# Three blocks of a two-layer kernel joined into one, with row products moved into the value products

## The chip, the cores and the metric

The kernel runs on one core of a Trainium2 chip. The metric is the device time of one execution in microseconds (us). Five engines run programs of their own and meet at semaphores: PE (TensorE, matrix products), DVE (VectorE), ACT (ScalarE), POOL (GpSimd) and SP (SyncE, which here only issues DMA transfers). PE's weight loads are shown apart as PEld.

## What is computed

Two layers act on 1024 tokens (2 sequences of 512) of width 512. The first adds attention and a gated feed-forward network to its input, the second a state-space mixer and a linear map with LoRA. Both normalise first.

```python
x = L0_attn_x                                   # (2, 512, 512), float32
xn = _layernorm(x)
q, k, v = proj(w_q), proj(w_k), proj(w_v)       # 32 heads of 16
attn = softmax(q @ k.T / 4)
inter = silu(xn @ gate_w.T * gate_scale) * (xn @ up_w.T * up_scale)      # width 1376
x = x + (attn @ v) @ w_o.T + inter @ down_w.T * down_scale
xn = _layernorm(x)
proj = xn @ in_proj_w.T                         # gate, x, B, C, dt
xBC = silu(conv1d(xBC, 4 taps) + conv_b)
y = ssd(xBC, dt, A, D)                          # 128 heads of 64, state 128, 8 groups, chunked scan
g = y * silu(gate)
g = g * rsqrt(mean(g * g over each group) + 1e-5) * norm_w
x = x + g @ out_w.T + (xn @ W.T + bias + lora(xn))
```

## The kernel before

**Products.** Each float32 product of weights and activations is made as three passes at reduced width: both operands are split into a high part (ACT copies, `hi`) and a rest (DVE or POOL subtracts, `lo`), and `product` issues hi times lo, lo times hi and hi times hi on PE (L156, L157, L158). Weights come by DMA into `raw` slots of a `Feed` and are split there (high L137 on ACT, rest L148 on DVE or POOL).

**Stages.** Three blocks follow one another, each with a program for each engine, and each ends with all five engines together. `emit_qkv` normalises the input and projects q, k and v. `emit_attention` runs the attention in a loop of 2 iterations of 4 quads (a quad is 4 heads in both sequences), with the gate and up products between its steps. `emit_ssm` first runs the program of `Down` (feed-forward down projection, attention output, second normalisation) and then 8 groups of the state-space part in 16 steps each; the last group differs a little, and behind it comes the output stage (`Output`, and the last products with `out_w`). On each engine the order of work is the order in which the code issues it; no scheduler moves it.

**The first normalisation** (`FirstNorm`) goes over 8 blocks of 128 tokens (`NTOK`). For block t DVE takes the moments (L242, L244), ACT a square root, DVE inverts it and forms a shift, ACT normalises in place, PE turns the block with four transposes (L210) into PSUM, ACT copies the high part (`xhi`, L227) and DVE the rest (`xlo`, L255). In an iteration t, ACT does the root of t, the normalisation of t-1 and the high part of t-2; DVE the moments of t, the scalars of t-1 and the rest of t-2.

**The projections.** A q or k tile is a weight block by both halves of the tokens (`half(n, b)`, 12 matmuls each). The first half of tile 0 begins once four blocks are split; the last three turns stand around it and the first half of tile 1 on PE. A finished q or k tile is copied to DRAM (`parts`, SP L427) and read back re-arranged as `stk_qs` and `stk_ks`, 12 transfers for each of four quads (`stack`, SP L329). SP issues these between the loads of the v weights (L129).

**The value products.** v takes 8 steps t of 12 matmuls each (`qkv_pv`). After each step PE does two row products of the first quads (`row_step`, L341, four matmuls in all), whose maxima DVE takes (L351). Row products have two buffers.

**The state-space part.** SP fetches running sums (`cumb`, 1 MB, `sums`) for each step; POOL splits weight rests (L148), decays the state (L1863), gates the output (L1875), adds up squares (L1881, L1885) and weighs inputs for the state (`ssm_xw`, L1852), which PE then needs (L1437). The sum of squares of a group goes over PE (L1421) to DRAM and back as a reciprocal root (`rstd`), by which the output stage scales the gated rows (DVE L2099), splits them (ACT L2066, DVE L2103) and multiplies them with `out_w`.

## Time and profile before

| | us |
|---|---|
| median of 3 runs | 2115.75 (2115.68 to 2117.44) |
| profiled execution, own time | 2119.49 |
| its span | 2117.8 |
| PE busy in it | 2077.2 (98%) |
| DVE, ACT, POOL busy | 1464.2, 1336.9, 868.3 |

The profile page tells one execution. It gives the busy time of each engine, then what each engine waited for, then single instructions in time. PE is the engine to follow here, and what matters is where it does not work or works at a lower clock.

### The profile page before, as it was taken

What the parts mean: (1) busy time and instruction counts of PE and PEld (TensorE: products, weight loads), DVE (VectorE), ACT (ScalarE), POOL (GpSimd) and SP (SyncE); (2) the same over time, 40 slices, a digit from 0 to 9 for tenths busy, and PEclk for the clock granted to TensorE, in tenths of its full rate; (3) what the DMA queues carried; (4) which work ended last, traced back from release to release, by engine and by line L of the source; (5) the groups of instructions that cost most, each with busy time, mean ns of one, the idle gap of its engine ahead of it and who ended that gap; (6) DMA issues with size and microseconds to landing.
All of it is one profiled execution on the core that took longest, in us unless ns stands there. A gap on an engine that the chain in (4) does not pass through costs nothing.

```text
span 2117.8 us, 33682 instructions
## 1 busy us (share of the span) xinstructions
PE 2077.2 (98%) x12040; PEld 1547.6 (73%) x12040; DVE 1464.2 (69%) x1811; ACT 1336.9 (63%) x2376; POOL 868.3 (41%) x762
## 2 busy tenths in 40 slices
PE   7899999999999999999999999999999999999999
PEld 5644444488877777777877777777777767888887
DVE  4466666286578778878778687787787775555555
ACT  4255555544678888878787887888778783233322
POOL 1001110131266666757667566676667681000000
PEclk9999999999999999999999999999999999999999
DMA  4422222142455545545455455455555457544552
GB/s 156 163 80 73 76 80 60 46 153 88 135 159 168 164 142 172 157 154 173 154 158 162 147 166 168 151 167 159 153 168 159 155 174 267 151 145 147 147 182 89
DMA packets 182781, 305.34 MB, mean 144 GB/s; under 512 B 20416, under 2 KB 96704, under 8 KB 182496
## 3 DMA queue, kind: packets, MB, share of 16 engines
q1 hardware_dynamic: 182624, 303.29, 46.3%
q8 instruction: 94, 1.54, 0.3%
q14 instruction: 63, 0.52, 0.1%
HBM read 249.90 MB, written 53.06 MB: 143 GB/s over the span
## 4 chain that ended last, share of the span: by engine, by line
PE 76%; ACT 1%; DVE 1%; POOL 1%; issue 1%; DMA 1%; DVEq 0%; SPq 0%; POOLq 0%; ACTq 0%
PE ssm_pp L156 16%; PE ssm_pp L158 15%; PE ssm_pp L157 15%; PE ssm_py L1458 5%; PE ssm_py L1453 4%; PE ssm_pstate L1437 4%; PE ssm_turn L1414 2%; PE ssm_py L158 1%; PE ssm_py L157 1%; PE ssm_py L156 1%; PE down_ps L156 1%; PE down_ps L158 1%; PE down_ps L157 1%; PE ssm_pp L1397 1%; PE ssm_pstate L158 1%; PE ssm_pstate L157 1%
## 5 line engine op out<-in xcount | busy, mean ns | idle before, releaser
L156 PE MATMUL ssm_pp<-xhi,ssm_lo 128*128 128x512 f32 x1192 | 478.8, 402 | 0.9 <-DVE ssm_bc L1697 0.4
L158 PE MATMUL ssm_pp<-xhi,ssm_hi 128*128 128x512 f32 x1192 | 465.5, 391 | 0.0
L157 PE MATMUL ssm_pp<-xlo,ssm_hi 128*128 128x512 f32 x1192 | 464.9, 390 | 0.0
L1583 ACT ACTIVATE ssm_sct<-ssm_cumb,ssm_gpar 128x128 f32<-128x128 f32 x1024 | 313.1, 390 | 71.5 <-DMA ssm_cumb<-dt_sums 50.3
L148 POOL TENSOR_TENSOR ssm_lo<-ssm_raw,ssm_hi 128x512 fp32r<-128x512 f32 x150 | 244.0, 1631 | 79.1 <-ACT ssm_hi L137 79.1
L156 PEld LDWEIGHTS ssm_pp<-xhi,ssm_lo 128*128 128x128 f32 x1192 | 223.6, 188 | 63.7 <-issue 18.8
L1697 DVE SCALAR_TENSOR_TENSOR ssm_xc<-ssm_pp,vectors,ssm_xc 128x1022 f32<-128x1022 f32 (+2 forms) x192 | 245.3, 1278 | 28.0 <-ACT ssm_xc L1537 23.4
L158 PEld LDWEIGHTS ssm_pp<-xhi,ssm_hi 128*128 128x128 f32 x1192 | 223.7, 188 | 48.1
L157 PEld LDWEIGHTS ssm_pp<-xlo,ssm_hi 128*128 128x128 f32 x1192 | 224.0, 188 | 42.6
L1732 DVE TENSOR_TENSOR ssm_sct<-ssm_sct,ssm_cbm 128x1024 f32<-128x1024 f32 x128 | 228.5, 1785 | 27.7 <-ACT ssm_sct L1590 27.7
L1875 POOL TENSOR_TENSOR ssm_go<-ssm_t,ssm_gt 128x512 f32<-128x512 f32 x128 | 165.0, 1289 | 171.8 <-DVE ssm_t L1768 171.8
L767 ACT ACTIVATE att_pt<-att_keys 128x512 f32<-128x512 f32 x256 | 143.8, 594 | 137.3 <-PE att_keys L657 137.1
L2066 ACT ACTIVATE xlo<-ssm_gt 128x1024 fp32r<-128x1024 f32 x64 | 67.8, 1060 | 239.4 <-PE ssm_turn L158 228.1
L351 DVE TENSOR_REDUCE stk_mx<-att_rows 128x2 f32<-128x1024 f32 x112 | 137.3, 1226 | 90.2 <-PE att_rows L341 90.2
L148 POOL TENSOR_TENSOR ffn_lo<-ffn_raw,ffn_hi 128x512 fp32r<-128x512 f32 x33 | 42.9, 1301 | 377.1 <-ACT ffn_hi L137 377.1
L1744 DVE TENSOR_TENSOR ssm_xp<-ssm_turn,ssm_gpar 128x512 f32<-128x512 f32 x128 | 87.9, 687 | 151.9 <-PE ssm_turn L1414 151.9
L1458 PE MATMUL ssm_py<-ssm_sct,ssm_xp 128*64 128x128 f32 x2048 | 184.3, 274 | 0.0
L2103 DVE TENSOR_TENSOR xlo<-ssm_gt,xlo 128x1024 fp32r<-128x1024 f32 x64 | 78.4, 1225 | 149.1 <-ACT xlo L2066 149.1
L1852 POOL TENSOR_TENSOR ssm_xw<-ssm_xp,ssm_gpar 128x512 f32<-128x512 f32 x96 | 127.1, 1324 | 107.7 <-DVE ssm_xp L1744 107.6
L1453 PE MATMUL ssm_py<-ssm_cecl,ssm_state 128*64 128x128 f32 x1536 | 154.1, 279 | 0.1
L1768 DVE SCALAR_TENSOR_TENSOR ssm_t<-ssm_xc,vectors,ssm_py 128x128 f32<-128x128 f32 x512 | 142.5, 338 | 5.3 <-PE ssm_py L1458 5.3
L1458 PEld LDWEIGHTS ssm_py<-ssm_sct,ssm_xp 128*64 128x64 f32 x2048 | 124.5, 137 | 24.3 <-DVE ssm_xp L1744 18.2
(287 smaller groups left out, 4148.3 us busy)
## 6 DMA issues: line engine op xcount, KB each, us to landing
ssm_cumb<-dt_sums SPq DMA_DIRECT2D x96, 1024.0 KB, 5.9
ssm_raw<-w SPq DMA_DIRECT2D x150, 256.0 KB, 5.4
gated<-ssm_go SPq DMA_DIRECT2D x128, 256.0 KB, 4.3
ssm_cumb<-dt_sums SPq DMA_DIRECT2D x32, 512.0 KB, 3.9
ssm_gt<-w SPq DMA_DIRECT2D x64, 256.0 KB, 2.7
ssm_xc<-gated SPq DMA_DIRECT2D x32, 512.0 KB, 4.1
ssm_sct<-gated SPq DMA_DIRECT2D x32, 512.0 KB, 4.2
ffn_raw<-w SPq DMA_DIRECT2D x37, 256.0 KB, 2.8
```

Source lines behind the costliest of these rows:

```text
L148: i = dve.tensor_tensor(lo, src, hi, ALU.subtract)
L156: pe.matmul(out, wlo, xhi, start=start, stop=False)
L157: pe.matmul(out, whi, xlo, start=False, stop=False)
L158: return pe.matmul(out, whi, xhi, start=False, stop=stop)
L767: act.activation(pt[:, kt % 2, PAIRED[u % HQ], :], keys[:, u % 2, :], ACT.Exp).then_inc(exp_done, 1)
L1453: pe.matmul(p_y[r * HP:(r + 1) * HP, s % 2, ct, :], state[:, ch % 2, h * HP:(h + 1) * HP], cecl[:, s % 2, h, :], start=True, stop=False)
L1458: mm = pe.matmul(p_y[r * HP:(r + 1) * HP, s % 2, ct, :], xp[:, s % 2, h * HP:(h + 1) * HP], sct[:, s % 2, h, :], start=(ch == 0), stop=True)
L1583: i = act.activation(sct[:, s % 2, h, :], cumb[:, s % 2, 0, h, :], ACT.Relu, scale=-1.0, bias=gpar[:, unit, 0, s % NTOK, h:h + 1])
L1697: i = dve.scalar_tensor_tensor(dst[:, :, sh:L], pp[:, e % 2, :, 0:L - sh], col(conv_col(g, e) + tap), dst[:, :, sh:L], ALU.mult, ALU.add)
L1732: dve.tensor_tensor(sct[:, s % 2, :, :], sct[:, s % 2, :, :], cbm[:, s % NTOK, :].unsqueeze(1).broadcast_to([P, HU, CS]), ALU.mult).then_i ...
L1768: i = dve.scalar_tensor_tensor(t2[:, s % 2, ct, :], xc[:, s // NTOK, ct, t * CS:(t + 1) * CS], col(g * (2 * CU) + (V_D + s // NTOK * CU + ...
L1875: pool.tensor_tensor(go[:, s % 2, :, :], t2[:, s % 2, :, :], gt[:, s // NTOK, :, t * CS:(t + 1) * CS], ALU.mult).then_inc(g_done, 1)
```

## The change

**One block.** `emit_qkv` becomes a class `Projections`, `emit_attention` a class `Attention`; their engine programs are called at the head of each engine's program in `emit_ssm`'s block, ahead of `Down`. In place of the two joint ends stand waits on semaphores: for all value copies on PE and POOL, for the last value sums and the last transfers of q and k parts on DVE, for these transfers on ACT; and in `Down` for the last copied attention sums on SP and, within its first tile, for that and the last gate and up tile on PE. Semaphores of the projections are given back (`retired`) before those of the state-space part are taken.

**First normalisation.** In an iteration ACT now does the high part of t-3, the normalisation of t-1 and the root of t; DVE the scalars of t-1, the moments of t and the rest of t-3. On PE six turns come first, the seventh stands within the first half of tile 0 and the eighth behind it.

**Order on SP.** The stacks move behind all loads of the v weights:

Here is SP in the projections; `qkv_raw` is a v weight, L427 a copy to DRAM, L329 the stacks. Before:

```order
L427 DMA qk_parts<-qk_lo 128x1024
L329 DMA stk_qs<-qk_parts 16x2x512 x6
L329 DMA stk_ks<-qk_parts 16x2x512 x6
L129 DMA qkv_raw<-w 128x512
L427 DMA qk_parts<-qk_hi 128x1024
L427 DMA qk_parts<-qk_lo 128x1024
L329 DMA stk_qs<-qk_parts 16x2x512 x6
L329 DMA stk_ks<-qk_parts 16x2x512 x6
L129 DMA qkv_raw<-w 128x512
```

And after, where the copy to DRAM has L423:

```order
L129 DMA qkv_raw<-w 128x512
L423 DMA qk_parts<-qk_hi 128x1024
L423 DMA qk_parts<-qk_lo 128x1024
L329 DMA stk_qs<-qk_parts 16x2x512 x6
L329 DMA stk_ks<-qk_parts 16x2x512 x6
L423 DMA qk_parts<-qk_hi 128x1024
L423 DMA qk_parts<-qk_lo 128x1024
L329 DMA stk_qs<-qk_parts 16x2x512 x6
L329 DMA stk_ks<-qk_parts 16x2x512 x6
```

Each stack (12 transfers) has moved from between two v weights to behind the last of them; the third now also stands behind two loads for the attention's gate and up weights.

**Row products.** The two row products of step t are done inside its value product, after the first 3 of 12 matmuls; only those of t = 0 still stand behind it. Here is PE at the end of the value products and the start of the attention. Before:

```order
L156 MATMUL qkv_pv<-qkv_hi,xlo 128x512
L157 MATMUL qkv_pv<-qkv_lo,xhi 128x512
L158 MATMUL qkv_pv<-qkv_hi,xhi 128x512
L341 MATMUL qkv_ps<-stk_ks,stk_qs 128x512 x4
L398 UNCONDITIONAL_BRANCH
L647 UNCONDITIONAL_BRANCH
L341 MATMUL att_rows<-stk_ks,stk_qs 128x512 x2
L657 MATMUL att_keys<-stk_qs,stk_ks 128x512 x2
```

After:

```order
L158 MATMUL qkv_pv<-qkv_hi,xhi 128x512
L341 MATMUL qkv_ps<-stk_ks,stk_qs 128x512 x4
L156 MATMUL qkv_pv<-qkv_hi,xlo 128x512
L157 MATMUL qkv_pv<-qkv_lo,xhi 128x512
L158 MATMUL qkv_pv<-qkv_hi,xhi 128x512
...
L156 MATMUL qkv_pv<-qkv_hi,xlo 128x512
L157 MATMUL qkv_pv<-qkv_lo,xhi 128x512
L158 MATMUL qkv_pv<-qkv_hi,xhi 128x512
L341 MATMUL att_rows<-stk_ks,stk_qs 128x512 x2
```

The last row products have moved ahead of nine matmuls of the last value step, and the attention's first row products follow the value product with no change of block between them.

**Running sums.** The transfer of `cumb` for a step waits for two ACT marks (`seg_done`, `cecl_done`) that show its buffer read, and no longer for the state of the step before (`st_done`).

**Last group and output.** SP loads the first inputs of the output stage at step 11 (before at 14) and asks for the first reciprocal roots at step 14 (before 15). Four weight rests go from POOL to DVE (`low_beside`). From step 6 on POOL weighs before it adds squares. ACT's last square and PE's last sums of squares move a few instructions into the output stage. Here is POOL near the end of the last group, before:

```order
L1852 TENSOR_TENSOR ssm_xw<-ssm_xp,ssm_gpar 128x512
L148 TENSOR_TENSOR ssm_lo<-ssm_raw,ssm_hi 128x512
L1863 TENSOR_TENSOR ssm_state<-ssm_state,ssm_cdec 128x512
L1875 TENSOR_TENSOR ssm_go<-ssm_t,ssm_gt 128x512
L1881 TENSOR_TENSOR ssm_sq<-ssm_sq 128x256
L1885 TENSOR_TENSOR ssm_sqs<-ssm_sq 128x128
L1852 TENSOR_TENSOR ssm_xw<-ssm_xp,ssm_gpar 128x512
```

And after:

```order
L1894 TENSOR_TENSOR ssm_state<-ssm_state,ssm_cdec 128x512
L1906 TENSOR_TENSOR ssm_go<-ssm_t,ssm_gt 128x512
L1883 TENSOR_TENSOR ssm_xw<-ssm_xp,ssm_gpar 128x512
L1912 TENSOR_TENSOR ssm_sq<-ssm_sq 128x256
L1916 TENSOR_TENSOR ssm_sqs<-ssm_sq 128x128
```

The weighing (L1852, now L1883) has moved ahead of the two additions of squares, and the weight rest (L148) is gone from the row.

The core of the diff:

```diff
 class FirstNorm: def scalar(self, act, feed):
-        for t in range(NTOK + 2):
+        for t in range(NTOK + 3):
+            if t >= 3:
+                self.high(act, t - 3)
+            if 1 <= t <= NTOK:
+                self.normalise(act, t - 1)
             if t < NTOK:
                 self.root(act, t)
-            if 1 <= t <= NTOK:
-                self.normalise(act, t - 1)
-            if t >= 2:
-                self.high(act, t - 2)
-            if 4 <= t < 4 + feed.begun:
-                feed.split_hi(act, 0, t - 4, 0)
+            if 3 <= t < 3 + feed.begun:
+                feed.split_hi(act, 0, t - 3, 0)
 ...
 SP of the projections
-                if n == 1:
-                    for s in parts_out[0:2]:
-                        sp.wait_ge(s, 32)
-                    sp.wait_ge(st.cleared, 2)
-                if 1 <= n < NB:
-                    st.stack(sp, c, 0, n - 1)
 ...
+            for s in parts_out[0:2]:
+                sp.wait_ge(s, 32)
+            sp.wait_ge(st.cleared, 2)
+            for i, n in enumerate(range(3 * KT - S - 2, nqk)):
+                st.stack(sp, c, 0, i)
                 parts(n)
             next_feed.begin_load(sp)
+            st.stack(sp, c, 0, NB - 2)
             st.neg_max(sp, 0, 0)
 ...
 PE of the projections
-            for t in range(NC + 1):
+            for t in range(NTOK - 2):
                 norm.turn(pe, t)
             pe.wait_ge(norm.lo_done, NC)
-            half(0, 0)
-            norm.turn(pe, NC + 1)
-            norm.turn(pe, NC + 2)
+            half(0, 0, range(KT // 2))
+            norm.turn(pe, NTOK - 2)
+            half(0, 0, range(KT // 2, KT))
+            norm.turn(pe, NTOK - 1)
             half(1, 0)
-            norm.turn(pe, NC + 3)
             pe.wait_ge(norm.lo_done, NTOK)
 ...
                     if t == 0:
                         pe.wait_ge(feed.lo_done, nqk + k + 1)
+                    if t > 0 and k == 1:
+                        maxima(t)
 ...
 heads of the engine programs of the attention
+            projections.values_out(pool)
             sweep(pool, body)
+            projections.values_out(pe)
             sweep(pe, body)
+            projections.vectors_in(dve)
+            projections.values_summed(dve)
+            projections.parts_written(dve)
+            projections.parts_written(act)
             act.wait_ge(scale_set, 3)
 ...
 Down
+            attention.last_sums_copied(sp)
             move_sums(sp, c, oe, att_moved, NIT - 1, NB - 1)
 ...
+                    if k == 0 and t == 4:
+                        attention.last_sums_copied(pe)
+                    if k == 0 and t == 6:
+                        attention.last_tile_read(pe)
 ...
 emit_ssm
             def sums(g, s):
-                after(sp, st_done, g * NS + (s - 1))
+                after(sp, seg_done, g * NS + (s - 1))
+                after(sp, cecl_done, g * NCA + (carry(s - 1) if s > 0 else -1))
 ...
+            for stage in stages:
+                stage.tensor(pe)
             down.tensor(pe, dt_product, first_tile)
 ...
+                    if last and s == 11:
+                        out.first_loads(sp)
                     if last and s == 14:
-                        out.first_loads(sp)
-                    if last and s == 15:
                         out.first_rstd(sp)
 ...
 POOL, a step
+                    ahead = last and s >= HALF_AT
+                    if ahead and behind(g, s, 1, last):
+                        weigh(*behind(g, s, 1, last))
                     if before(g, s, 2):
                         add_squares(*before(g, s, 2))
-                    if behind(g, s, 1, last):
+                    if not ahead and behind(g, s, 1, last):
                         weigh(*behind(g, s, 1, last))
 ...
 PE, output stage
-        last_squares()
         for n in range(G * NB):
 ...
-                for bank in (0, 2, 4, 1, 3, 5, 7):
+                for bank in (0, 2, 4, 1, 3, 5):
                     gated(n, bank)
+                last_squares()
+                gated(n, 7)
```

## Rows read from the trace of the kernel before

**Rows 1.** The page's first part: busy us, share of the span, instructions.

```profile
PE 2077.2 (98%) x12040; PEld 1547.6 (73%) x12040; DVE 1464.2 (69%) x1811; ACT 1336.9 (63%) x2376; POOL 868.3 (41%) x762
```

**Rows 2.** Waits of PE, whole span: engine, line, waited for; us total, times, longest.

```profile
PE qkv_pv L210 <- ACT stk_v L222: 9.6, 2, 7.5
...
PE ssm_pstate L1437 <- POOL ssm_xw L1852: 3.9, 5, 1.2
...
PE down_ps L156 <- PEq L552: 1.2, 1, 1.2
```

**Rows 3.** Stretches: us, busy PE PEld DVE ACT POOL, PE clock, DMA share, GB/s.

```profile
18.73:21.95 3.22, 3.13 (x10) 2.24 (x9) 1.79 (x5) 2.11 (x5) 1.28 (x1) 1.00 0.29 82
75.00:81.00 6.00, 5.91 (x15) 3.84 (x16) 3.62 (x4) 0.82 (x2) 0.00 (x0) 0.50 1.02 388
108.00:116.00 8.00, 8.00 (x30) 4.11 (x26) 3.57 (x3) 4.18 (x8) 0.00 (x0) 0.57 0.66 191
404.80:408.80 4.00, 4.00 (x14) 1.28 (x13) 1.90 (x2) 2.10 (x4) 1.28 (x1) 0.57 0.27 71
620.00:1690.00 1070.00, 1069.66 (x7101) 838.82 (x7098) 839.62 (x1074) 863.53 (x1588) 709.77 (x612) 1.00 0.51 160
1761.70:1767.30 5.60, 5.58 (x13) 4.44 (x14) 4.25 (x4) 1.01 (x2) 0.00 (x0) 0.51 0.87 303
```

**Rows 4.** Head, in time: start, us, engine line op out<-in [idle before <-releaser].

```profile
18.73 0.69 DVE L255 TENSOR_TENSOR xlo<-qkv_ps,xhi 128x512 fp32r<-128x512 f32 x1 [1.36 <-ACT xhi L227]
...
19.48 0.79 PE L156 MATMUL qkv_ps<-xhi,qkv_lo 128*128 128x512 f32 x1
...
27.97 0.60 PE L210 MATMUL qkv_ps<-ident,stk_v 128*128 128x128 f32 x4
29.98 0.50 PE L156 MATMUL qkv_ps<-xhi,qkv_lo 128*128 128x512 f32 x1 [1.41 <-DVE xlo L255]
```

**Rows 5.** Value products and start of the attention, in time, three engines.

```profile
71.61 0.50 PE L156 MATMUL qkv_pv<-qkv_hi,xlo 128*128 128x512 f32 x1 [1.90 <-DVE qkv_lo L148]
...
75.09 0.80 PE L156 MATMUL qkv_pv<-qkv_hi,xlo 128*128 128x512 f32 x1 [2.50 <-DVE qkv_lo L148]
...
77.51 2.36 DVE L351 TENSOR_REDUCE stk_mx<-qkv_ps 128x2 f32<-128x1024 f32 x2 [1.03 <-PE qkv_ps L341]
...
82.22 0.74 PE L341 MATMUL qkv_ps<-stk_ks,stk_qs 48*128 48x512 f32 x4
...
104.03 0.60 ACT L513 ACTIVATE stk_v<-qkv_pv 128x512 f32<-128x512 f32 x1 [3.02 <-PE qkv_pv L158]
...
107.65 0.51 PE L341 MATMUL att_rows<-stk_ks,stk_qs 48*128 48x512 f32 x2 [3.00 <-PEq L398]
```

**Rows 6.** PE at the middle of the attention, in time.

```profile
404.52 0.50 PE L657 MATMUL att_keys<-stk_qs,stk_ks 50*128 50x512 f32 x1 [0.79 <-ACT att_pt L767]
```

**Rows 7.** Feed-forward down stage, in time, DVE and PE.

```profile
426.23 3.35 DVE L953 RECIPROCAL down_ratio<-down_ratio 128x512 f32<-128x512 f32 x1 [1.83 <-DMA down_ratio<-att_sums]
...
436.92 1.21 DVE L291 TENSOR_TENSOR stk_ks<-ffn_h,stk_qs 128x1024 fp32r<-128x1024 f32 x1
...
438.27 0.47 PE L156 MATMUL down_ps<-ffn_hi,stk_ks 128*128 128x512 f32 x1
```

**Rows 8.** Last group and output stage, in time: POOL, SP's queue, DVE, PE.

```profile
1739.67 1.74 POOL L1881 TENSOR_TENSOR ssm_sq<-ssm_sq 128x256 f32<-128x256 f32 x1
...
1751.17 0.73 POOL L1881 TENSOR_TENSOR ssm_sq<-ssm_sq 128x256 f32<-128x256 f32 x1
...
1751.70 0.45 SPq L1973 DMA_DIRECT2D ssm_raw<-rstd  x1
...
1757.20 1.53 DVE L2099 TENSOR_TENSOR ssm_gt<-ssm_xc,ssm_raw 128x1024 f32<-128x1024 f32 x1 [4.21 <-DMA ssm_raw<-rstd]
1757.70 1.05 PE L1421 MATMUL ssm_pstate<-ssm_sqs,ones 128*32 128x512 f32 x4 [0.97 <-POOL ssm_sqs L1885]
1761.72 0.80 PE L156 MATMUL ssm_pp<-xlo,xhi 128*128 128x512 f32 x1 [2.96 <-DVE xlo L2103]
```

More of the change, by code:

```diff
@@ L831, in sync, with sums @@
         def sync(sp):
-            def attention(k):
+            def sums(k):
                 if k == 1:
@@ L842, in sync @@
                 sp.wait_ge(s, NQUAD // 2 * 2 * HQ * 16)
-            attention(0)
+            sums(0)
             for n in range(FIRST + 5, OUT + KT):
@@ L1608, in lora_high @@
                                    ).then_inc(marks.lora_hi, 1)
+            for stage in stages:
+                stage.scalar(act)
             down.scalar(act)
@@ L1825, in body @@
                         lora_low()
+                    for r in (real(g, e, AHEAD) for e in at(s - 1, last) if last and e >= NE):
+                        if exists(r, last):
+                            low_beside(r)
                     for e in single(s - 1, last):
@@ L1890, in low @@
                 feed.split_lo(pool, gg * GT, rr)
+            for stage in stages:
+                stage.gpsimd(pool)
             down.gpsimd(pool)
@@ L1902, in body @@
                         r = real(g, e, AHEAD)
-                        if is_tile(e) and exists(r, last):
+                        if is_tile(e) and exists(r, last) and not (last and e >= NE):
                             low(r)
@@ L2186, in build @@
                     oe = ssm_feed.raw[:, 0:2, :]
-                    emit_attention(nc, c, w, xhi, xlo, st, hid, ffn_feed, ffn_done, att_moved, oe)
-                if upto <= 1: return
+                    attention = Attention(nc, cs, cy, c, w, xhi, xlo, st, hid, ffn_feed, ffn_done, att_moved, oe,
+                                          projections)
                 dt_feed.raw = h[:, 6:7, 0:512]
```

133 lines of the change are left out of this document (71 added, 62 removed).

## Prediction, made before the changed kernel had run

> **What bounds the kernel now.** I read the busy time first, then PE's waits, then stretches with PE's clock, then single instructions where PE had waited. PE works 2077.2 of the 2117.8 us of the span [rows 1], so about 40.6 us are idle, and 9.6 of these are two waits at the very start, 7.5 the longer, for the first normalised block [rows 2]. Between 620 and 1690 us, which is most of the state-space part, PE is busy 1069.66 of 1070.00 us at full clock [rows 3]: there is 0.34 us to be had. So the change can only gain at the places where PE waits or runs at its lower clock: the head, the value products, the start of the attention, the down stage, and the last group with the start of the output. A lower clock costs time that no wait shows. In three stretches of 5.6 to 8 us the granted clock is 0.50 to 0.57 [rows 3], near the lower of its two levels (1.2 against 2.4 GHz), with PE busy throughout.
>
> **Head (normalisation and first tiles).** Before, each block of 128 tokens takes 3.22 us, and in this time DVE is busy 1.79 and ACT 2.11 (a weight split included) [rows 3]: neither is full, they hand on to each other, and DVE waits 1.36 us for each high part [rows 4]. The new order puts the high part, which needs only PE, ahead of what needs DVE's scalars, so the two overlap. The period should fall to what ACT is busy, about 2 us (bounds 1.8 and 3.2). The rests come one iteration later in the order (t-3), so of the gain on four blocks (4 x 1.2) most is given back at once: I work the first four through and get the first product at 17.6 instead of 19.48 [rows 4], 1.9 earlier. Behind it PE no longer catches up with the normalisation: the last turn (0.60) and the wait (1.41) between the first half of tile 1 and the second half of tile 0, from 27.97 to 29.98 [rows 4], become nothing, because the remaining four blocks need 4 x 2 = 8 us and PE has about 8.5 us of other work there (19.48 to 27.97). 1.9 + 2.0 = **3.9 us** (2.5 if the period falls to 2.5 only; 5 if the first product comes at 16.7).
>
> **Value products.** PE waits 1.90 us at 71.61 and 2.50 at 75.09 for split v weights [rows 5]. The weights lie behind 12 stack transfers each on SP's queue; after, no v weight is behind any. Both waits go: 4.4. From 75 to 81 the clock is 0.50 with PE busy 5.91 us [rows 3], so half of this, 3.0, is the price of the low clock, which follows these waits. New: the first row products wait for the first stack, which SP now issues after the last v weight; I expect it to land 1 to 2 us before PE wants it, and 0.3 us for the copy of the last tile to end. And the second pair of row products stands only three matmuls, about 0.7 us, behind the first, while DVE needs 2.36 us for two maxima [rows 5] and there are two buffers: 2.36 less 0.7 and less part of the row products' own 0.74 [rows 5] is 1.0 to 1.6 of waiting, once; I take 1.3. From then on a value step is 12 matmuls long and covers its maxima. 4.4 + 3.0 - 1.6 = **5.8 us** (3 if the clock still falls, 6.8 if nothing new waits).
>
> **From projections to attention.** PE stands 3.00 us at the change of block [rows 5]. What remains true without the block: PE must have the last value step copied (ACT, 0.60 [rows 5]). The last row products now stand inside that step, so their maxima end with it and don't come on top. 3.00 less 0.75 (the copy and two semaphores) is 2.25. Behind it the clock is 0.57 from 108 to 116 with PE busy 8.00 [rows 3]: at most 8.00 x 0.43 = 3.4 us; I take 2.75, since ACT and DVE are also starting up there. I take off 0.6 for the first exponentials, which PE now reaches sooner. 2.25 + 2.75 - 0.6 = **4.4 us** (1.7 if the clock falls as before, 5 by the upper end).
>
> **Attention to down.** PE stands 1.2 us at this change of block [rows 2]. But what follows is paced by DVE: it starts at 426.23 when the attention's sums arrive, and ends the hidden tile that PE takes next at 436.92 + 1.21 = 438.13; PE's product with it is at 438.27 [rows 7]. PE that comes 1.2 us sooner waits 1.2 us more there. Only SP's copy of the last sums moves by about a quarter of a microsecond, an estimate from its place behind the joint end. **0.3 us** (-0.6 to 1.3: nothing returned, or the new waits of PE in the first tile taken up in full).
>
> **Running sums.** SP's transfers may go out earlier; PE has 0.34 us of waiting in 1070 us there [rows 3], so the gain is 0 and the only question is harm (below).
>
> **Last group and output.** PE waits 3.9 us five times for the weighed inputs of POOL [rows 2]. The weighing now goes before two additions of squares, and one weight rest in POOL's way is DVE's: I take 3.2 back. The last squares stand at the head of the output stage: PE waits 0.97 for them at 1757.70 and then 2.96 for the first scaled rows, at 1761.72 [rows 8]. The scaled rows wait 4.21 us for the reciprocal roots, a transfer issued only at 1751.70, behind the last-but-one copy of gated rows [rows 8]; asked for one step sooner, it is no longer late, and the last squares find six products in front of them. Of 3.93 us 0.3 is left: 3.6. The low clock from 1761.70 (0.51, busy 5.58 [rows 3]) costs up to 2.7; I take 2.4 back. Minus 0.2 for DVE's four splits. 3.2 + 3.6 + 2.4 - 0.2 = **9.0 us** (5 if POOL's waits stay and half of the rest, 10.5 if all goes).
>
> A rule bears on POOL's part. One square addition takes 1.74 us at 1739.67 and 0.73 at 1751.17 [rows 8], the same shape, the latter with little going on on DVE. The Trainium skill, "SBUF — State Buffer", section "Who interferes with whom", says that a DVE instruction with two SBUF inputs contends with GpSimd's reads, and the trace agrees in direction (1.74 against 0.73). By that rule the four splits moved to DVE do not free POOL for their whole time; that case is a rival below, by rows.
>
> **Rivals.**
>
> *The clock falls again at a new, short wait.* Two new waits of about a microsecond remain where PE was slow before (the second row products, the start of the attention). For it: at 404.52 PE waits 0.79 us for an exponential [rows 6], and from 404.8 to 408.8 its clock is 0.57 [rows 3]. Against it: the two waits before the low clock at 75 add up to 4.4 us. If it falls at one, 2.75 or 3.0 us return: 2095; at both, 2098. The Trainium skill, "TensorE: Matmul & The Clock Gate", section "What's actually happening", says that the throttled state is the default and that activity releases it; the rows at 404.52 agree that a short pause can be enough (0.57 after 0.79 us).
>
> *The last group is bound by DVE and POOL.* The four splits now stand on DVE, where the state-space steps run too, and slow POOL's additions from 0.73 towards 1.74 us [rows 8]; then the waits for weighed inputs stay (3.2) and the last squares are late by about 0.8 us more. This part gives 5 instead of 9: 2096.
>
> *Waits take the place of the joint ends.* The ends of blocks may cost nothing beyond what the semaphores cost as well: PE still stands 3 us before the attention and the clock falls as before. The 4.4 and 0.3 go: 2097.
>
> *Slower: running sums crowd out weights.* The transfers, up to 1 MB each, now go out as soon as their buffer is read, and can stand ahead of a weight tile on the 16 DMA engines, busy 0.51 in the mean there [rows 3]. PE in this part has no slack at all, so a weight late by 0.21 us in each of 112 steps (7 groups of 16) takes back 112 x 0.21 = 23.5 us, all the gain; from 0.25 us each the kernel is slower, 2120. Against it: the mean load is half, and the time before the sums are needed is a whole step.
>
> **How the numbers follow.** 3.9 + 5.8 + 4.4 + 0.3 + 9.0 = 23.4 us. The profiled execution took 2119.49 (3.74 above the median; its span and 1.7 around it), so its like should take 2096.1; taken from the median of 2115.75 it is 2092.35, and I predict **2092 us**. Chances: this case 0.55; the clock falls again 0.25 (2095 to 2098); the last group bound by DVE and POOL 0.10 (2096); waits in place of joint ends 0.05 (2097); slower 0.02; something that eats the gain up to no difference 0.03. The parts' best ends add up to 28.6 (2087), their worst, 2.5 + 3 + 1.7 - 0.6 + 5, to 11.6 (2104); all worst at once is unlikely, so the range is 2087 to 2102. About 0.2% (4.2 us) is what a measurement of this kernel can tell from no change; every case but the last two is beyond it: faster 0.95, same 0.03, slower 0.02.
>
> **What would show it right or wrong.** Head: DVE's `xlo` rows 2 us apart, the first product near 17.6, no wait between the first halves and the second. Value products: no wait for v weights, clock 1.00 throughout, one wait of 1 to 1.5 us at the second row products. Attention: PE's first row products within a microsecond of the last value product, and the clock at 1.00 after them. Down: the DVE chain begins within 0.5 us of where it would have by the earlier gains, and PE waits about 1.2 us more for hidden tiles. Last group: waits for `ssm_xw` under 1 us in all, the transfer of the reciprocal roots issued before the copy of the last-but-one gated rows, no wait of about 3 us at the first output products, clock 1.00. The forecast is wrong if the stacks land late, so that the first row products wait for them for more than 1 us; if any of the three low-clock stretches stays; or if the state-space part between its first and its last group is longer than before.

## The result

The changed kernel takes 2093.21 us, median of 4 runs (2092.92 to 2095.57), against 2115.72 for the kernel before (2115.20 to 2117.44): a ratio of 0.9892, 95% interval 0.9878 to 0.9906. The forecast was 2092, with a range of 2087 to 2102. Its profiled execution took 2095.57 us with a span of 2093.9, and the one before 2119.49 with 2117.8: both are longer than their kernel's median, by 2.4 and 3.8 us.

First the busy times and then PE's waits over the whole span of the changed kernel (engine, line, waited for: us in total, times, longest):

```profile
PE 2070.1 (99%) x12040; PEld 1544.0 (74%) x12040; DVE 1467.9 (70%) x1815; ACT 1337.1 (64%) x2376; POOL 869.5 (42%) x758
```

```profile
PE qkv_pv L210 <- ACT stk_v L222: 9.5, 4, 7.6
PE att_keys L659 <- ACT att_pt L771: 1.9, 5, 0.8
...
PE qkv_ps L341 <- DVE stk_mx L351: 0.8, 2, 0.6
...
PE att_rows L341 <- ACT stk_v L509: 0.7, 1, 0.7
PE ssm_pp L156 <- DVE xlo L2141: 0.6, 1, 0.6
PE ssm_pstate L1455 <- ACT ssm_sqs L1620: 0.6, 1, 0.6
```

Against [rows 1] PE does the same 12040 matmuls in 7.1 us less busy time (2077.2 to 2070.1); the same matmuls with fewer stretches of low clock, so most likely that is clock given back. Its idle time falls from 40.6 to 23.8 us, 16.8 less. Together these are the 23.9 us by which the span is shorter. The waits for `ssm_xw`, for the joint ends and for the v weights are gone from the list; short ones for maxima (L351), for the last v copy and, within the last group, for a copy of squares (L1620) stand in their place.

PE's matmuls come in nearly the same order in both kernels, so the same matmul can be found in both traces, and its two starting times show how much has been gained up to there. Here are six such places of the kernel before, on PE in time (start, us, engine line op out<-in; a seventh is the start of the attention, at 107.65 [rows 5]):

```profile
68.19 0.39 PE L156 MATMUL qkv_pv<-qkv_hi,xlo 128*128 128x512 f32 x1
...
117.63 0.40 PE L657 MATMUL att_keys<-stk_qs,stk_ks 50*128 50x512 f32 x2
...
416.33 0.47 PE L156 MATMUL down_ps<-ffn_hi,stk_ks 128*128 128x512 f32 x1 [1.24 <-PEq L552]
...
1670.37 0.39 PE L156 MATMUL ssm_pp<-xhi,ssm_lo 128*128 128x512 f32 x1
...
1756.34 0.39 PE L158 MATMUL ssm_py<-dtw_hi,ssm_hi 128*128 128x512 f32 x1
...
2112.99 0.39 PE L158 MATMUL ssm_turn<-xlo,xhi 128*128 128x512 f32 x1
```

And the same matmuls in the changed kernel:

```profile
64.10 0.39 PE L156 MATMUL qkv_pv<-qkv_hi,xlo 128*128 128x512 f32 x1
...
97.01 0.50 PE L341 MATMUL att_rows<-stk_ks,stk_qs 48*128 48x512 f32 x2 [0.69 <-ACT stk_v L509]
...
105.18 0.40 PE L659 MATMUL att_keys<-stk_qs,stk_ks 50*128 50x512 f32 x2
...
401.16 0.50 PE L156 MATMUL down_ps<-ffn_hi,stk_ks 128*128 128x512 f32 x1
...
1655.21 0.39 PE L156 MATMUL ssm_pp<-xhi,ssm_lo 128*128 128x512 f32 x1
...
1737.85 0.39 PE L158 MATMUL ssm_py<-dtw_hi,ssm_hi 128*128 128x512 f32 x1
...
2089.06 0.39 PE L158 MATMUL ssm_turn<-xlo,xhi 128*128 128x512 f32 x1
```

The kernel was profiled a second time (e8 below); the last column but one has the same subtraction with that profile.

| part of the sum | gained up to its end, us | its own gain | with e8's profile | forecast |
|---|---|---|---|---|
| head, to the first value product | 68.19 - 64.10 = 4.09 | 4.1 | 4.4 | 3.9 |
| value products, to the start of the attention less its wait (3.00 before, 0.69 after) | 107.65 - 97.01 = 10.64 | 4.2 | 5.8 | 5.8 |
| that wait, and the first 8 us of the attention | 117.63 - 105.18 = 12.45 | 2.3 + 1.8 = 4.1 | 4.1 | 4.4 |
| rest of the attention and joint end to the down stage | 416.33 - 401.16 = 15.17 | 2.7 | 2.9 | 0.3 |
| down stage and state-space part to the last group | 1670.37 - 1655.21 = 15.16 | 0.0 | 0.0 | 0 |
| last group | 1756.34 - 1737.85 = 18.49 | 3.3 | 2.8 | 3.0 |
| start of the output, to the last matmul | 2112.99 - 2089.06 = 23.93 | 5.4 | 5.4 | 6.0 |

The clock in five stretches of the changed kernel, for [rows 3] (us, busy PE, PEld, DVE, ACT, POOL, granted clock, DMA share, GB/s):

```profile
70.10:73.60 3.50, 3.42 (x8) 2.44 (x9) 2.29 (x3) 0.00 (x0) 0.00 (x0) 0.51 0.57 170
96.50:108.00 11.50, 10.33 (x47) 5.14 (x47) 6.62 (x10) 7.54 (x14) 1.02 (x2) 1.00 0.10 25
388.00:400.00 12.00, 11.10 (x52) 4.63 (x44) 3.44 (x4) 8.14 (x15) 1.29 (x1) 1.00 0.22 59
600.00:1670.00 1070.00, 1069.66 (x7106) 838.36 (x7106) 839.78 (x1077) 867.92 (x1596) 710.40 (x614) 1.00 0.49 159
1737.00:1745.00 8.00, 7.36 (x31) 4.66 (x30) 5.70 (x5) 2.36 (x4) 3.41 (x4) 1.00 0.92 291
```

The low stretches at the start of the attention, in its middle and at the output are gone, and one of 3.4 us is new, at the second row products (0.51). The state-space part is busy 1069.66 of 1070.00 us, as before.

### The profile page after: what moved, and what is told of

Same layout as the page of the kernel before. It is cut to its first block, busy times and chain, and to the rows that moved or that the text cites. A ratio compares the mean times of both kernels' runs of the same rounds, so it can differ in the third digit from the quotient of the medians.

```text
span 2093.9 us, 33789 instructions
## 1 busy us (share of the span) xinstructions
PE 2070.1 (99%) x12040; PEld 1544.0 (74%) x12040; DVE 1467.9 (70%) x1815; ACT 1337.1 (64%) x2376; POOL 869.5 (42%) x758
## 4 chain that ended last, share of the span: by engine, by line
PE 93%; ACT 2%; DVE 1%; POOL 1%; issue 1%; DMA 1%; SPq 0%; DVEq 0%; ACTq 0%; POOLq 0%
PE ssm_pp L156 16%; PE ssm_pp L158 15%; PE ssm_pp L157 15%; PE att_gu L684 6%; PE ssm_py L1476 5%; PE ssm_py L1471 4%; PE ssm_pstate L1455 4%; PE att_pv L670 3%; PE ssm_turn L1432 2%; PE att_rows L341 2%; PE att_keys L659 2%; PE ssm_py L158 1%; PE ssm_py L157 1%; PE ssm_py L156 1%; PE down_ps L156 1%; PE down_ps L158 1%
## 5 line engine op out<-in xcount | busy, mean ns | idle before, releaser
L156 PE MATMUL ssm_pp<-xhi,ssm_lo 128*128 128x512 f32 x1192 | 478.8, 402 | 0.9 <-DVE ssm_bc L1718 0.4
L157 PE MATMUL ssm_pp<-xlo,ssm_hi 128*128 128x512 f32 x1192 | 464.9, 390 | 0.0
L148 POOL TENSOR_TENSOR ssm_lo<-ssm_raw,ssm_hi 128x512 fp32r<-128x512 f32 x146 | 239.1, 1643 | 76.9 <-ACT ssm_hi L137 76.9
L156 PEld LDWEIGHTS ssm_pp<-xhi,ssm_lo 128*128 128x128 f32 x1192 | 223.6, 188 | 63.7 <-issue 18.8
L157 PEld LDWEIGHTS ssm_pp<-xlo,ssm_hi 128*128 128x128 f32 x1192 | 224.0, 188 | 42.6
L351 DVE TENSOR_REDUCE stk_mx<-att_rows 128x2 f32<-128x1024 f32 x112 | 137.3, 1226 | 89.0 <-PE att_rows L341 89.0
L148 POOL TENSOR_TENSOR ffn_lo<-ffn_raw,ffn_hi 128x512 fp32r<-128x512 f32 x33 | 42.9, 1302 | 371.5 <-ACT ffn_hi L137 371.5
L1883 POOL TENSOR_TENSOR ssm_xw<-ssm_xp,ssm_gpar 128x512 f32<-128x512 f32 x96 | 130.4, 1358 | 109.5 <-DVE ssm_xp L1765 109.5
L1471 PE MATMUL ssm_py<-ssm_cecl,ssm_state 128*64 128x128 f32 x1536 | 154.2, 279 | 0.8 <-issue 0.8
```

Of the source, the lines that this page charges most:

```text
L148: i = dve.tensor_tensor(lo, src, hi, ALU.subtract)
L156: pe.matmul(out, wlo, xhi, start=start, stop=False)
L157: pe.matmul(out, whi, xlo, start=False, stop=False)
L1471: pe.matmul(p_y[r * HP:(r + 1) * HP, s % 2, ct, :], state[:, ch % 2, h * HP:(h + 1) * HP], cecl[:, s % 2, h, :], start=True, stop=False)
```

## The experiments

All but e5 start from the changed kernel. Beside them the kernel before was run again, 27 times, and it has no steady time: its mean granted clock went from 0.994 to 0.997, with spans of 2116.7 to 2117.6 us at 0.994 and of 2113.5 to 2113.6 at 0.997. Its median falls among the long executions in one group of runs and among the short ones in the next (2115.7 to 2118.9 us), so a difference to it can be off by 3 us. The changed kernel's own median was 2093.21 and, run again (e8), 2093.37. So the table also gives each time less 2093.3, and from the traces how much later PE's last matmul starts than in e8's profile, where no low clock follows the head. The last two columns are the ones to compare; where they differ by a microsecond or two, no run decides.

| run | time, us | before, run beside it | difference | time less 2093.3 | last matmul less e8's |
|---|---|---|---|---|---|
| e1, old head | 2099.05 | 2118.86 | -19.8 | +5.8 | +3.8 |
| e2, old place of the stacks | 2101.28 | 2118.86 | -17.6 | +8.0 | +7.7 |
| e3, old place of the row products | 2095.72 | 2118.86 | -23.1 | +2.4 | +2.0 |
| e4, second row products later | 2092.33 | 2118.86 | -26.5 | -1.0 | -1.2 |
| e5, joining alone | 2116.06 | 2116.32 | -0.3 | +22.8 | +18.7 |
| e6, old start of the output | 2098.25 | 2116.32 | -18.1 | +5.0 | +4.5 |
| e7, e4 and the table load early | 2091.87 | 2116.32 | -24.5 | -1.4 | -2.5 |
| e8, changed kernel again | 2093.37 | 2116.32 | -23.0 | +0.1 | 0 |
| e9, splits on POOL | 2094.58 | 2115.68 | -21.1 | +1.3 | +0.1 |
| e10, weighing behind | 2094.81 | 2115.68 | -20.9 | +1.5 | +1.3 |
| e11, old wait of the sums | 2095.07 | 2115.68 | -20.6 | +1.8 | +0.5 |

**Old head (e1).**

```diff
 def scalar(self, act, feed):
-        for t in range(NTOK + 3):
-            if t >= 3:
-                self.high(act, t - 3)
+        for t in range(NTOK + 2):
+            if t < NTOK:
+                self.root(act, t)
 ...
```

DVE and PE have their old order back as well.

> The changed kernel (2093.2 us) with the first normalisation and the first turns on PE in their old order. Theory: the handing-on between ACT, DVE and PE sets the head, and nothing behind it gives the gain back: the first value product comes at 68.2 us again instead of 64.1, and the time is 2093.2 + 4.1 = 2097.3 us, all of it before 68 us. Rival: what stands behind the head (v weights, stacks, maxima) is paced by transfers that do not move with it, so part of the 4.1 is given back there: 2094 to 2096 us.

The first value product starts at 68.07 us, 3.97 later than in the first profile of the changed kernel (64.10) and 4.30 later than in e8, so the head carries what was said. The last matmul starts 2.2 us later than in the first profile and 3.8 later than in e8. What lies between these two is no transfer: it is the clock at the second row products. The waits there are the same in all three profiles (0.8 us, the longer 0.6), and in e1 and e8 the clock stays up behind them, as this stretch of e1 shows:

```profile
73.00:78.00 5.00, 4.36 (x20) 2.85 (x20) 3.35 (x3) 0.60 (x1) 0.00 (x0) 1.00 0.62 189
```

So the theory holds: nothing behind the head gives its gain back. The median is 5.8 us above the changed kernel's, and the profiled execution is the shortest of its four; where the others lose the rest is not shown.

**Old place of the stacks (e2).**

```diff
 def parts(n):
 ...
+                if 1 <= n < NB:
+                    st.stack(sp, c, 0, n - 1)
 ...
-            for i, n in enumerate(range(3 * KT - S - 2, nqk)):
-                st.stack(sp, c, 0, i)
+            for n in range(3 * KT - S - 2, nqk):
                 parts(n)
 ...
```

> The changed kernel with the stack transfers between the loads of the v weights again; the row products stay inside the value products. Theory: the place on SP's queue made PE wait for v weights; the two waits come back (4.4 us) with a stretch of low clock behind them (1.6 to 3.4 us), and the short waits at the second row products (0.8 us) and their low clock (1.6 us) go: 2093.2 + 4.4 + 2.5 - 2.4 = 2097.7 us. Rival: the waits for v weights went because of the earlier head or the moved row products: no wait over 1 us for v weights, 2092 to 2094 us.

On PE in time, and the stretch around and behind the second wait:

```profile
67.12 0.50 PE L156 MATMUL qkv_pv<-qkv_hi,xlo 128*128 128x512 f32 x1 [1.80 <-DVE qkv_lo L148]
...
70.50 0.80 PE L156 MATMUL qkv_pv<-qkv_hi,xlo 128*128 128x512 f32 x1 [2.40 <-DVE qkv_lo L148]
```

```profile
69.60:79.80 10.20, 9.30 (x23) 5.72 (x24) 6.63 (x6) 1.63 (x3) 0.00 (x0) 0.50 0.79 302
```

The two waits of [rows 5] are back almost to the tenth (1.80 and 2.40 against 1.90 and 2.50), with half the clock for 10.2 us from within the second one on. The kernel is 8.0 us slower by the medians and 7.7 by the traces; 4.5 were expected, with a shorter low stretch, and less 1.6 for a low clock that e8's profile does not have. The size was off, but the theory holds: it was the queue's order that PE waited for.

**Old place of the row products (e3).**

```diff
-                    if t > 0 and k == 1:
-                        maxima(t)
 ...
                     pe.wait_ge(qk_l, nqk)
-                    maxima(t)
+                maxima(t)
```

> The changed kernel with the row products of each step behind its value product again, the stacks still behind the v weights. Theory: the row products of step 1 then come twelve matmuls (2.7 us) behind those of step 0, longer than two maxima (2.4 us), so the waits of 0.2 and 0.6 us and the low clock from 70.1 to 73.6 (1.6 us) go; the last maxima then stand ahead of the attention and cost 1 to 1.7 us there: 2093.2 - 2.4 + 1.3 = 2092.1 us. Rival: the place inside the product carries the gain at the start of the attention: PE stands 1.7 us longer there and its clock falls behind it (2.7 us): 2093.2 - 2.4 + 4.4 = 2095.2 us.

PE at the first row products of the attention, and two stretches behind it:

```profile
94.42 0.50 PE L341 MATMUL att_rows<-stk_ks,stk_qs 48*128 48x512 f32 x2 [2.31 <-DVE stk_mx L351]
```

```profile
95.10:101.90 6.80, 6.80 (x20) 3.94 (x18) 2.59 (x3) 3.45 (x5) 0.00 (x0) 0.50 0.01 2
392.00:395.50 3.50, 3.50 (x13) 1.12 (x5) 1.56 (x2) 1.77 (x3) 1.28 (x1) 0.51 0.32 95
```

Both accounts were half right. Where they differed, the rival saw it: without the block PE still stands 2.31 us before the attention, now for the last two maxima, and the clock falls behind it for 6.8 us. The value products, on the other side, lose their waits and have no low clock. The sum is a loss, 2.4 us by the medians and 2.0 by the traces, near the rival's 2095.2; of the 2.0, about 1.5 is a low clock in the middle of the attention (the second stretch), a place that the edit does not touch. So joining the blocks is worth little at the start of the attention unless the last maxima are out of the way.

**Second row products later (e4).**

```diff
-                    if t > 0 and k == 1:
+                    if t > 0 and k == (3 if t == 1 else 1):
```

> The changed kernel with one thing moved: the row products of step 1 stand after nine of its twelve matmuls instead of three. Theory: the wait there (0.2 and 0.6 us) and the low clock from 70.1 to 73.6 (1.6 us) go, nothing else changes: 2093.2 - 2.4 = 2090.8 us. Rival: the clock falls at the next short wait instead (start of the attention, where PE waits 0.7 and 0.4 us), and 1.6 to 3.4 us return: 2092.4 to 2094 us.

The wait for maxima at `qkv_ps` L341 is gone from PE's list, and no other stretch of low clock has come up. The span is 2091.2 us, 2.7 less than in the first profile of the changed kernel, where 2.4 were expected. But against e8, where the waits are there and the clock stays up, only 0.6 us are gained between the first value product and the attention, and the medians differ by 1.0. The time, 2092.33, is nearer to the rival's 2092.4 than to the theory's 2090.8, but the rival's low clock is nowhere in the trace. So the theory holds for the waits; the 1.6 us of clock are won only where the clock would have fallen.

**Joining alone (e5).** The kernel before with only the one block and the waits that replace the joint ends; every other edit is taken back.

> The kernel before with the joining alone: one block, waits in place of the two joint ends; normalisation, SP's order, row products, running sums, last group and output as before. Theory: of the 3.0 us at the start of the attention only about 0.7 go, since PE then waits for the last two maxima (2.3 us, as with the old place of the row products), with a low clock behind it as before, and the 1.2 us at the down stage go in full: 2.0 us faster than before. First rival: 2.25 and 1.2 us go and the clock stays up at the attention (2.75): 6 us faster. Second rival: waits cost what the joint ends cost, within 0.5 us of before.

The difference to before is nothing that can be measured (ratio 0.9996, interval 0.9986 to 1.0006). The start of the attention, and two stretches of its profile:

```profile
106.08 0.67 PE L341 MATMUL att_rows<-stk_ks,stk_qs 48*128 48x512 f32 x2 [2.31 <-DVE stk_mx L351]
```

```profile
106.25:113.05 6.80, 6.80 (x20) 3.89 (x21) 2.76 (x5) 3.45 (x5) 0.00 (x0) 0.50 0.10 23
388.00:412.00 24.00, 22.93 (x106) 9.58 (x104) 5.67 (x7) 15.90 (x29) 3.34 (x4) 1.00 0.12 34
```

3.00 us of waiting became 2.31, and the clock falls as before. At the down stage the 1.24 us are gone. In the last group and at the output PE waits about as long as before: 4.4 us for `ssm_xw`, 1.8 for the last squares and 1.8 for the first scaled rows, against 3.9, 1.0 and 3.0 [rows 2, 8]. The profiled execution is 3.4 us faster than the median of all ten; in it the clock did not fall in the middle of the attention (1.00 from 388 to 412) and at the output. So the trace shows the 1.9 us of waiting gone that the theory named, and the median shows nothing; its interval, 3.0 us faster to 1.3 slower, holds the theory's 2.0 as well as the second rival. The first rival is out.

**Old start of the output (e6).**

```diff
-                    if last and s == 11:
+                    if last and s == 14:
                         out.first_loads(sp)
-                    if last and s == 14:
+                    if last and s == 15:
                         out.first_rstd(sp)
 ...
+        last_squares()
         for n in range(G * NB):
 ...
```

ACT's last square and DVE's first splits of scaled rows have their old order back as well.

> The changed kernel with the start of the output as before: first loads at step 14, reciprocal roots asked for at step 15, last square and last sums of squares ahead of the output products; POOL's order and the four splits stay changed. Theory: the reciprocal roots' late transfer set the start of the output; PE waits 3 to 4 us in all there again and its clock is low behind it (2 to 3 us): 5.5 us slower than the changed kernel, none of it before the last group's end. Rival: with POOL's additions out of the way the squares and the gated rows come earlier anyway, and most of it stays gained: under 2.5 us slower.

The first output products on PE, and the stretch behind:

```profile
1736.76 1.05 PE L1439 MATMUL ssm_pstate<-ssm_sqs,ones 128*32 128x512 f32 x4 [0.72 <-POOL ssm_sqs L1917]
1741.69 0.62 PE L156 MATMUL ssm_pp<-xlo,xhi 128*128 128x512 f32 x1 [3.88 <-DVE xlo L2141]
```

```profile
1741.90:1745.30 3.40, 3.40 (x9) 2.62 (x9) 3.40 (x4) 0.79 (x2) 0.00 (x0) 0.50 0.60 165
```

PE waits 0.72 + 3.88 = 4.6 us again, and the low clock is back, for half the time of before. The kernel is 4.9 us slower than the changed one run beside it (2093.37). The theory holds, with 5.5 expected.

**Row products later and the table load early (e7).** ACT loads the table for its exponentials at the first of them, 1.28 us, in the changed kernel between the first keys of the attention and their exponentials. One exponential on a spare column now stands ahead of the sixth v copy.

```diff
             for t in range(NTOK):
+                if t == NTOK - 3:
+                    act.activation(norm.rs[:, 0:1], norm.rs[:, 0:1], ACT.Exp)
                 act.wait_ge(v_sum, t + 1)
```

> The changed kernel with the row products of step 1 after nine matmuls (as in the run with the second rows later) and, new, one exponential on a column of 128 values during the value products, so that ACT's table load of 1.28 us lies there and not behind the attention's first keys. Theory: PE's wait of 0.4 us for the first exponentials goes and the state-space part is untouched: 2.4 + 0.4 = 2.8 us faster than the changed kernel. Rival: ACT is late for the attention by other work (the v copy at 96.4), the 0.4 us stay: 2.4 us faster, as without it.

ACT, in time:

```profile
84.32 1.28 ACT L509 ACT_TABLE_LOAD   x1
...
95.00 1.09 ACT L773 ACTIVATE att_pt<-att_keys 128x512 f32<-128x512 f32 x2 [0.90 <-PE att_keys L661]
```

PE's wait of 0.4 us for the first exponentials is gone (1.5 us in 4 waits instead of 1.9 in 5). By the starting times it is worth more: from the attention's first row product to the transpose behind its second pair of keys it takes 3.70 us in e4 (94.57 to 98.27) and 2.54 here (94.15 to 96.69), 1.2 us less. It is the fastest kernel of the study: 2091.87 (2091.05 to 2092.74) against 2093.37 (2092.61 to 2094.02) for the changed one run beside it, 1.5 us. The ranges overlap by a little; that it is faster rests on the traces too, where its span is 2.5 us shorter than e8's (2.8 was expected against the changed kernel).

**The changed kernel again (e8).**

> The changed kernel itself, in one call with the others. If the places where the clock falls are set by the order of work alone, its profile has again one low stretch, at the second row products, and it is 22.5 us faster than before. If the same wait sometimes is and sometimes is not followed by a low clock (the run with the old head had the same waits of 0.2 and 0.6 us and full clock behind them), the low stretch can be missing or stand elsewhere, and the time differs by 1.5 to 3.5 us.

The stretch with the waits of 0.2 and 0.6 us at the second row products:

```profile
69.80:73.20 3.40, 3.36 (x14) 2.36 (x14) 2.25 (x2) 0.55 (x1) 0.00 (x0) 1.00 0.54 175
```

Same kernel, same waits, and 1.00 instead of 0.51. The span is 1.6 us shorter (2092.3). The seven matched places are at 63.77, 95.12, 103.30, 399.08, 1653.14, 1736.32 and 2087.52 us; against the first profile 0.3 us are won in the head, 1.6 at the value products, and 0.5 are lost in the last group. That is how far two profiles of one kernel differ part by part.

**POOL and DVE in the last group (e9, e10).**

```diff
 e9: POOL takes the four weight rests again
-                        if is_tile(e) and exists(r, last) and not (last and e >= NE):
+                        if is_tile(e) and exists(r, last):
 ...
 e10: POOL weighs behind the additions again
-                    ahead = last and s >= HALF_AT
+                    ahead = False
```

In e9 the four `low_beside` on DVE are gone as well.

> The changed kernel with the four weight rests of the last group on POOL again (1.27 us each), POOL's weighing still ahead of the additions of squares. Theory: the order of the weighing carries the 3.3 us that the last group gained, since the rest comes ahead of the output and the weighing, but the additions, 2.4 to 3.1 us a step, now come behind: under 1 us slower than the changed kernel. Rival: POOL had no room and each rest still pushes the weighing: PE waits for weighed inputs 1 to 1.3 us in three or four steps again, 3 to 4 us slower.

> The changed kernel with POOL's weighing behind the additions of squares again, the four weight rests still on DVE. Theory: the weighed inputs then come 2.4 to 3.1 us later in each step from 6 on, and PE waits for them again: 2 to 3.5 us slower than the changed kernel in the last group. Rival: with the rests gone from POOL the weighing is early enough in either place: under 0.5 us slower.

From a state-space product of the last but one group (L156, at 1653.14 in e8 and 1652.28 and 1652.69 here) to the last matmul it takes 434.38 us in e8 (433.85 in the first profile of the changed kernel), 435.33 in e9 and 436.10 in e10. So the rests cost about 1.0 us on POOL and the place of the weighing 1.7, each to about the half microsecond by which two profiles of the changed kernel differ here; with both as they were it was 3.3 (2.8 against e8). In e10 the waits for weighed inputs are back:

```profile
PE ssm_pstate L1455 <- POOL ssm_xw L1883: 3.1, 4, 1.6
```

3.1 us of waiting cost 1.7; of e8's other waits in the last group, 1.1 us at L1471 and 0.4 for `dtw_lo` are not in e10's list. For e9 the theory holds (about 1 us, 1.3 by the medians; its last matmul is only 0.1 us later than e8's, since its head ended 1.1 earlier); for e10 it does in kind, with 1.7 us (1.5 by the medians) a little under its range.

**Old wait of the running sums (e11).**

```diff
-                after(sp, seg_done, g * NS + (s - 1))
-                after(sp, cecl_done, g * NCA + (carry(s - 1) if s > 0 else -1))
+                after(sp, st_done, g * NS + (s - 1))
```

> The changed kernel with the transfers of the running sums waiting for the state of the step before again. Theory: PE waits 0.34 us in 1070 us there, so nothing is to be had: within 1 us of the changed kernel, and equal times from group to group in the state-space part. Rival: the earlier transfers crowd out weights or, the other way, free ACT earlier: over 2 us either way, as a drift that grows from group to group.

A product in the seventh group (L157) starts at 1594.29 us, and at 1594.31 in e8: in these two traces the earlier transfers neither gain nor harm, and nothing drifts. The last group takes 0.5 us more than in e8, as much as two profiles of the changed kernel differ there (434.38 and 433.85). The median is 1.8 us above the changed kernel's, though, with a range (2094.49 to 2096.32) above e8's, where within 1 us was expected. The traced execution is the shortest of the four and shows no place for it, and the changed kernel was not run beside it: this stays open.

## Why the prediction was right, and where it was not

The sum was 23.4 us. The first two profiles show 23.9, the medians 22.5, and with e8 as the changed kernel's profile it is 25.5. So that the sum came out to half a microsecond is in part luck: its terms for the clock (3.0, 2.75 and 2.4) were read from one execution of the kernel before, 3.74 us above the median from which they were then taken, and the mean clock of that kernel's executions goes from 0.994, as in this one, to 0.997. Against the first profile two terms were off, in opposite directions; against e8 only one was.

**Head: right.** The rests (`xlo`) come 1.9 us apart, and the first product starts at 17.11 (17.6 was said), with no wait between the tiles' halves (of the 9.6 us read as waits for the first block, 2.1 stand at 18.27 us, before a later one; no term rests on it):

```profile
13.83 0.66 DVE L255 TENSOR_TENSOR xlo<-qkv_ps,xhi 128x512 fp32r<-128x512 f32 x1
...
15.72 0.66 DVE L255 TENSOR_TENSOR xlo<-qkv_ps,xhi 128x512 fp32r<-128x512 f32 x1
```

One thing in the head was not looked at. PE's first products take 0.63 us each, as in the low stretch behind 70.18, and 0.39 from some moment on: from 22.4 us in this profile, from 19.6 in e9. With the same head, e9's first value product starts at 62.71 instead of 64.10. So up to 1.4 us of this part differ between executions.

**Value products: 4.2 instead of 5.8 in the first profile, 5.8 in e8.** The waits for v weights went, as e2 confirms from the other side, and the new wait was smaller than said (0.2 + 0.6 against 1.3). What failed in the first profile is "clock 1.00 throughout": behind a wait of 0.63 us at 70.18 it was 0.51 for 3.4 us.

```profile
70.18 0.80 PE L341 MATMUL qkv_ps<-stk_ks,stk_qs 48*128 48x512 f32 x2 [0.63 <-DVE stk_mx L351]
```

This is the first rival, at one of its two places and at 1.6 us instead of 3.0. The first profile has it; e8 does not. In e8 the sum fits to the tenth, though its pieces do not quite: the two waits (4.4) and the low clock (3.0) less the new waits (0.24, 0.20 and 0.63) would be 6.3.

**Projections to attention: right in size, 4.1 against 4.4.** The wait is 0.69 (0.75 was said) and the clock stays at 1.00. But the text put the gain down to the joining, with the last maxima as a remark. e3 and e5 show that they belong together: the joining alone leaves 2.31 us and the low clock, and only with the last row products inside the value product does the copy of 0.60 end last.

**Attention to down: 2.7 instead of 0.3, the term that was mis-sized most.** Two things were missed. First, 1.5 us stand in the middle of the attention: the same 0.8 us wait for an exponential is there in both kernels, at 404.52 before [rows 6], but behind it the clock fell before and not after. That the change did this is not shown: in e3 the clock fell there with most of the change in place, in e5 it stayed up without most of it. Second, the joint end's 1.24 us did come back, in e5 as well. The step that failed is that DVE, started by the arriving sums, paces the down stage, so that PE coming sooner would only wait longer. POOL and DVE there, in the kernel before, the changed one and e5:

```profile
429.18 1.29 POOL L148 TENSOR_TENSOR ffn_lo<-ffn_raw,ffn_hi 128x512 fp32r<-128x512 f32 x1 [3.64 <-ACT ffn_hi L137]
...
429.50 2.05 DVE L291 TENSOR_TENSOR stk_ks<-ffn_h,stk_qs 128x1024 fp32r<-128x1024 f32 x1
```

```profile
414.05 1.29 POOL L148 TENSOR_TENSOR ffn_lo<-ffn_raw,ffn_hi 128x512 fp32r<-128x512 f32 x1 [3.63 <-ACT ffn_hi L137]
...
415.12 1.31 DVE L291 TENSOR_TENSOR stk_ks<-ffn_h,stk_qs 128x1024 fp32r<-128x1024 f32 x1
```

```profile
424.91 1.29 POOL L148 TENSOR_TENSOR ffn_lo<-ffn_raw,ffn_hi 128x512 fp32r<-128x512 f32 x1 [3.63 <-ACT ffn_hi L137]
...
426.03 1.25 DVE L291 TENSOR_TENSOR stk_ks<-ffn_h,stk_qs 128x1024 fp32r<-128x1024 f32 x1
```

DVE's split begins 0.32 us after POOL's in the first and 1.07 and 1.12 after it in the others, because the sums come 0.8 us later by PE's time: DVE's chain starts 426.23 - 416.33 = 9.9 us behind PE's first product before [rows 7], and 411.84 - 401.16 = 10.7 after. Yet it ends 1.08, 1.09 and 1.08 us after POOL's split has ended, in all three, and beside no work of POOL's such a split takes 1.21 us [rows 7]. So before, DVE had been held up by POOL's split, and there was room for the sums to come later: the end goes by POOL's split, which moves with PE, and the late sums cost nothing. (The Trainium skill, "SBUF — State Buffer", section "Who interferes with whom", says that a DVE instruction with two SBUF inputs contends with a GpSimd instruction that reads SBUF, and that issue order decides who blocks; the 2.05 against 1.25 us agree.) That is read from three traces; no run moved POOL's split by itself.

**Running sums: right, 0.0**, by the traces of the changed kernel and of e11; e11's median leaves 1.8 us unexplained, on the side of a gain by the change. The slower rival has nothing for it.

**Last group and output: 8.8 against 9.0 (8.2 in e8).** No wait for `ssm_xw` is left (e10 brings it back); other waits of 0.6, 0.8 and 0.4 us stand in the last group. SP asks for the reciprocal roots directly behind one copy of gated rows and ahead of the next two, 4.7 us before them, and DVE scales without a wait:

```profile
1728.01 0.38 SPq L1304 DMA_DIRECT2D gated<-ssm_go  x1
1728.49 0.45 SPq L2009 DMA_DIRECT2D ssm_raw<-rstd  x1
1733.16 0.36 SPq L1304 DMA_DIRECT2D gated<-ssm_go  x1
```

The rival that DVE and POOL bind the last group did not come. At the first output products 0.65 us are left instead of 0.3.

Of the rivals the first came in part, in one profile of two. The third, that waits take the place of the joint ends at the same cost, is near what the joining alone does at the start of the attention (e5: 2.31 of 3.00 us left, and the low clock); the place of the row products kept it from coming (e3). At the down stage it is wrong, also in e5.

## What to carry to other kernels

Taking away a joint end of all engines is worth only what no other wait takes over: 3.00 us became 2.31 when the joint end went alone, and 0.69 when the last work before it was moved inside a product as well, while the other joint end's 1.24 went in full. For a part that is bound by one engine, find the same instruction of it in both traces and subtract its starting times; this splits a gain of 1% into its parts. But take two profiles of each kernel: two of the changed one differ by 0.3 to 1.6 us in three of seven parts. And a wait has a price of its own and another for the clock behind it, which can be the larger (0.6 and 1.6 us at the second row products) and does not come each time.

## What the runs showed of the hardware that was not expected

The clock behind a short wait is not set by the wait alone. The waits of 0.2 and 0.6 us at the second row products are in seven profiles (the changed kernel, e1, e6, e8, e9, e10, e11), and the low clock followed in one. The wait of 0.8 us in the middle of the attention is in all thirteen, and the low clock followed in two (before and e3). Behind the head, seven single waits are of 2.3 us or more: in the kernel before at 75, 108 and 1761 us, in e2 at the v weights, in e3 and e5 at the attention, and in e6 at the output. At each of them the clock fell, during the wait or just behind it, for 3.4 to 10.2 us. Between these lie waits of 1.6 to 2.0 us, and they differ: behind 1.90 us at 71.61 in the kernel before the clock stayed up until the next wait, behind 1.95 us at 71.81 in e5 it fell, and at e5's output, behind 1.83 and 1.77 us, it stayed up. The kernel before, and then two stretches of e5:

```profile
71.60:74.10 2.50, 0.98 (x3) 0.49 (x3) 1.22 (x1) 0.56 (x2) 0.00 (x0) 1.00 1.03 395
...
72.20:78.90 6.70, 4.75 (x12) 2.46 (x11) 4.23 (x5) 2.14 (x3) 0.00 (x0) 0.50 1.02 414
1754.60:1762.00 7.40, 5.62 (x24) 3.93 (x25) 6.94 (x7) 2.90 (x4) 0.00 (x0) 1.00 0.86 300
```

One profile can therefore mislead by 1.6 us for a short wait, both ways. What decides at a short wait stays open; the program is the same in the first profile of the changed kernel and in e8.

DVE and POOL can hold each other up: a split of 128x1024 took 1.21 us on DVE with POOL idle [rows 7] and 2.05 when it began 0.32 us behind a split of POOL's, and it then ended 1.08 us after POOL's.
